# First cross-attention: the first 1,792 keys get a scale of their own and are made ahead of the values, and later keys are made two supers ahead

## The reference

```python
Qp = query @ Wq + bq
K = _l2norm(key @ Wk + bk)
V = value @ Wv + bv
Q = _l2norm(Qp)
... (16 heads of 8)
scores = jnp.einsum('bhqd,bhkd->bhqk', Q, K) * SCALE
attn = jax.nn.softmax(scores, axis=-1)
out = jnp.einsum('bhqk,bhkd->bhqd', attn, V)
out = out @ Wo + bo
x = out + Qp
mu = jnp.mean(x, axis=-1, keepdims=True)
var = jnp.mean((x - mu) ** 2, axis=-1, keepdims=True)
return (x - mu) / jnp.sqrt(var + LN_EPS) * ln_gamma + ln_beta
```

## Time and profile before

| | us |
|---|---|
| median of 3 runs | 663.24 (662.68 to 671.8) |
| the profiled execution | 663.12, span 661.3 |
| first and last exponential of this stage | start 34.25, end 99.60 |
| PE, DVE, ACT, POOL busy over the whole span | 513.6, 434.1, 299.6, 132.1 |
| mean granted clock of TensorE | 0.853 |

### The profile page before, as it was taken

How to read it: one execution, slowest core, us unless ns; L and a number is a source line. 1 busy time by engine, 2 the same in 40 slices (tenths; PEclk the granted TensorE clock), 3 DMA queues, 4 the chain that set the end, 5 groups by cost and what they waited for, 6 DMA issues and landing times. The chain is left out here.

```text
span 661.3 us, 11985 instructions
## 1 busy us (share of the span) xinstructions
PE 513.6 (78%) x4815; PEld 324.5 (49%) x4815; DVE 434.1 (66%) x828; ACT 299.6 (45%) x367; POOL 132.1 (20%) x197
## 2 busy tenths in 40 slices
PE   8799996788889997438995594782578488999857
PEld 5456673575355564313442263472456335556546
DVE  6744325856967955744999999925556596785243
ACT  2578881425557685111654560020112164768611
POOL 2111000000000000204688999400100000000000
PEclk9989997989899999556998587795569679999959
DMA  8364481563200000001022035052300150000000
GB/s 218 72 185 117 128 321 57 173 181 80 94 2 2 1 3 1 3 0 50 0 84 111 0 147 124 5 116 55 127 1 1 31 256 1 2 2 2 2 0 3
DMA packets 17674, 45.59 MB, mean 69 GB/s; under 512 B 4281, under 2 KB 13674, under 8 KB 16778
## 3 DMA queue, kind: packets, MB, share of 16 engines
q1 hardware_dynamic: 17556, 44.72, 22.3%
q0 software_dynamic: 64, 0.11, 0.1%
HBM read 34.28 MB, written 8.29 MB: 64 GB/s over the span
## 5 line engine op out<-in xcount | busy, mean ns | idle before, releaser
L251 POOL TENSOR_TENSOR rstd<-rstd,minus_half 64x1 f32<-64x1 f32 x20 | 11.8, 589 | 420.3 <-DVE rstd L259 420.3
L1497 ACT ACTIVATE ring<-psum,l3x_gain_columns 128x1024 f32<-128x1024 f32 x49 | 54.4, 1114 | 23.2 <-PE psum L1389 23.2
L1497 ACT ACTIVATE ring<-psum,l1x_gain_columns 128x1024 f32<-128x1024 f32 x49 | 54.4, 1114 | 22.4 <-PE psum L1389 22.4
L1403 PE MATMUL psum<-ring,values 128*32 128x128 f32 x1568 | 62.7, 279 | 0.4 <-ACT ring L1497 0.4
L934 ACT ACTIVATE ring<-psum,l0x_key_scale 128x1024 f32<-128x1024 f32 x49 | 52.1, 1114 | 8.2 <-PE psum L827 8.2
L1403 PEld LDWEIGHTS psum<-ring,values 128*32 128x32 f32 x1568 | 37.0, 109 | 28.1 <-issue 24.7
L1602 DVE TENSOR_REDUCE l1x_tops<-psum 128x1 f32<-128x448 f32 x64 | 36.7, 619 | 10.2 <-PE psum L1378 10.1
L1602 DVE TENSOR_REDUCE l3x_tops<-psum 128x1 f32<-128x448 f32 x64 | 36.7, 619 | 10.2 <-PE psum L1378 10.1
L3186 DVE MAX8 l2x_best<-values 128x8 f32<-128x6272 f32 x6 | 40.1, 6691 | 0.1
L3194 DVE MATCH_REPLACE8 values<-l2x_best,values 128x6272 f32<-128x6272 f32 x6 | 40.1, 6675 | 0.0
L827 PE MATMUL psum<-l0x_Q_stack,wide 96*128 96x256 f16 x196 | 29.8, 281 | 4.2 <-ACT ring L934 2.1
(11 more groups left out here) (778 smaller groups left out, 1080.7 us busy)
## 6 DMA issues: line engine op xcount, KB each, us to landing
wide<-keys_aside SPq DMA_DIRECT2D x54, 224.0 KB, 3.8
experts<-in_experts SPq DMA_DIRECT2D x1, 4608.0 KB, 13.5
experts<-in_experts SPq DMA_DIRECT2D x1, 4096.0 KB, 15.3
keys_aside<-ring SPq DMA_DIRECT2D x7, 448.0 KB, 2.5
keys_aside<-experts SPq DMA_DIRECT2D x6, 448.0 KB, 3.2
ring<-in_ctx_tiles SPq DMA_DIRECT2D x1, 2352.0 KB, 9.3
experts<-in_experts SPq DMA_DIRECT2D x1, 2048.0 KB, 7.8
ctx_t<-in_ctx_t SPq DMA_DIRECT2D x3, 672.0 KB, 7.4
```

What stands on the lines that cost most here:

```text
L1403: last = nc.tensor.matmul(ps[32 * quarter:32 * quarter + 32, O_BANK, 128 * half:128 * half + 128], mem.values[:, at:at + 32], probs[:, t % ...
L1497: nc.scalar.activation(probs[:, t % PROBS, :].rearrange("p (b n) -> p b n", b=2), ps[:, pair:pair + 2, :], ACT.Exp, scale=exp_gain[:, :]). ...
```

## The change

- `AHEAD` is 2: super u's tiles carry the keys of super u+2, and `norms(u+2)` comes at its tile 6 (before: at tile 0).
- Supers 0 and 1 get a power of two of their own, from the first piece of the context (`bounds(0)`, `power_of_two(0)`); supers 2 to 6 get the second, whose bound PE computes inside the loop, after tile 4's keys.
- Keys 0 and 1 come ahead of the values on PE, and keys 2 and 3 ahead of the last three; ACT and not DVE writes high parts of super 1.
- The queries' high rows of `Q_stack` are copied by 8 DVE copies; before, SP moved them by 8 transfers.
- Super 0's stack: SP issues 8 transfers of high parts as soon as those are there, POOL the 4 of low parts.
- From super 2 on DVE does, per super: high, low, high, low, `take_norms(u)`, `scale_keys(u)`; SP does `stack_keys(u)`, then `turn_norms(u)`.
- The bounds for level 1 move to the end of DVE's list, and on PE from t = 38 to t = 42.

The diff, cut to its core:

```diff
-    AHEAD = 3
+    AHEAD = 2
     blocks = [(g, block_row) for g in range(G) for block_row in range(3)]
-    OF_POOL = [(g, 2) for g in range(2)]
+    OF_POOL = [(g, 1) for g in range(G)]
...
+                stack_keys(0)
                 turn_norms(0)
-                stack_keys(0)
+                stack_keys(1)
                 turn_norms(1)
-                stack_keys(1)
                 load_pack(mem, sp, "l1x")
-                turn_norms(2)
-                stack_keys(2)
-                for u in range(3, SUPERS):
+                for u in range(2, SUPERS):
                     stack_keys(u)
                     turn_norms(u)
...
                     pe.wait_ge(squares_ready, 2 * u + 2)
                     if u:
                         pe.wait_ge(rows_ready, u)
+                    if u == 2:
+                        pe.wait_ge(*dve_done.at("key_gain1"))
...
-                values(0)
+                keys(0)
                 pe.wait_ge(*dve_done.at("xnT"))
                 nc.tensor.matmul(ps[0:T, 3, 192:320], xnT[:, :], mem.w(pack, "Wq"), start=True, stop=True)\
                     .then_inc(*pe_done.mark("Qp"))
+                keys(1)
+                values(0)
+                norms(0)
+                pe.wait_ge(*dve_done.at("bounds0"))
...
                 values(2)
-                pe.wait_ge(*dve_done.at("Qn"))
-                nc.tensor.transpose(ps[0:C, 3, 320:384], Qn[:, :], ident[0:T, 0:T]).then_inc(*pe_done.mark("QT"))
-                keys(0)
-                keys(1)
                 values(3)
-                norms(0)
+                keys(2)
+                keys(3)
                 pe.wait_ge(mem.loaded["ctx2"], 16)
...
                 norms(1)
-                keys(4)
                 pe.wait_ge(*act_done.at("Q_stack"))
-                pe.wait_ge(queries_stacked, 16 * 2 * G)
+                pe.wait_ge(*dve_done.at("Q_stack"))
...
-                        if j == 0 and u + 2 < SUPERS:
-                            norms(u + 2)
-                        if j in (2, 4) and u + AHEAD < SUPERS:
+                        if u + AHEAD < SUPERS and j in (2, 4):
                             keys(2 * (u + AHEAD) + j // 4)
-
-                pe.wait_ge(*dve_done.at("key_gain"))
+                        if u + AHEAD < SUPERS and j == 6:
+                            norms(u + AHEAD)
+                        if tile == 4:
+                            pe.wait_ge(*dve_done.at("bounds1"))
+                            pe.wait_ge(rows_ready, 2)
+                            nc.tensor.matmul(ps[:, 0, 0:C], mem.ones[0:CTX + 1, :], bound_rows[:, :], start=True,
+                                             stop=True).then_inc(*pe_done.mark("key_bound1"))
...
-                    if t == 38:
+                    if t == 42:
                         gains.pe_bounds(pe, 1)
...
-                for u in range(3):
-                    copy_values(u)
                 square(0)
                 square(1)
-                copy_values(3)
+                copy_values(0)
+                act.wait_ge(*dve_done.at("key_gain0"))
+                high(0)
+                high(1)
+                copy_values(1)
+                copy_values(2)
                 act.wait_ge(*dve_done.at("Q_parts"))
                 for g in range(G):
                     ins = nc.scalar.activation(Q_stack[64:96, g, :], Q_low[32 * g:32 * g + 32, :], ACT.Identity)
                 ins.then_inc(*act_done.mark("Q_stack"))
-                copy_values(4)
-                act.wait_ge(*dve_done.at("key_gain"))
-                high(0)
-                high(1)
-                copy_values(5)
+                copy_values(3)
                 square(2)
-                copy_values(6)
                 square(3)
-                square(4)
+                high(2)
+                high(3)
+                for u in range(4, SUPERS):
+                    copy_values(u)
...
-                pool.wait_ge(high_ready, 2)
+                pool.wait_ge(low_ready, 2)
...
+                def bounds(n, lo, hi):
+
+                    step(v.tensor_reduce(piece_tops[:, n:n + 1], mem.ctx_top[:, lo:hi], AX_X, ALU.max))
+                    v.tensor_scalar(bound_rows[:, :], keys_abs[:, :], piece_tops[:, n:n + 1], None, ALU.mult)\
+                        .then_inc(*dve_done.mark(f"bounds{n}"))
...
+                def power_of_two(n, row):
+                    dve.wait_ge(*pe_done.at(f"key_bound{n}"))
+                    step(v.tensor_reduce(bound[:, :], row, AX_X, ALU.max))
+                    step(v.tensor_scalar(power[:, :], bound[:, :], 1e-30, None, ALU.max))
+                    bits = power[:, :].bitcast(I32)
+                    step(v.tensor_scalar(bits, bits, EXPONENT_BITS, None, ALU.bitwise_and))
+                    step(v.reciprocal(inverse[:, :], power[:, :]))
+                    v.tensor_scalar(exp_gain[:, n:n + 1], power[:, :], 2.0 ** -13 / QUERY_GAIN, None, ALU.mult)
+                    v.tensor_scalar(key_gain[:, n:n + 1], inverse[:, :], 2.0 ** 13, None, ALU.mult)\
+                        .then_inc(*dve_done.mark(f"key_gain{n}"))
...
+                bounds(0, *CTX_PIECES[0])
...
+                power_of_two(0, ps[:, 3, 64:192])
                 dve.wait_ge(*pool_done.at("q_rsqrt"))
                 v.tensor_scalar(Qn[:, :], Qp[:, :], q_rsqrt[:, :], None, ALU.mult)\
                     .then_inc(*dve_done.mark("Qn"))
-                context_top(1)
+                dve.wait_ge(*dve_done.at("key_gain0"))
+                low(0)
...
+                low(1)
+                take_norms(0)
+                for g in range(G):
+                    for block_row in range(2):
+                        ins = v.tensor_copy(Q_stack[32 * block_row:32 * block_row + 32, g, :], Q_high[32 * g:32 * g + 32, :])
+                ins.then_inc(*dve_done.mark("Q_stack"))
+                low(2)
+                low(3)
+                context_top(1)
+                scale_keys(0)
+                take_norms(1)
...
-                dve.wait_ge(*dve_done.at("key_gain"))
-                low(0)
-                low(1)
-                step(v.tensor_scalar(exp_gain[:, :], power[:, :], 2.0 ** -13 / QUERY_GAIN, None, ALU.mult))
-                scale_keys(0)
-                for n in range(2, 2 * AHEAD):
-                    high(n)
-                    low(n)
-                    if n == 3:
-                        take_norms(1)
+                bounds(1, CTX_PIECES[0][1], SUPERS)
+                power_of_two(1, ps[:, 0, 0:C])
+                dve.wait_ge(*dve_done.at("key_gain1"))
                 scale_keys(1)
+                for u in range(2, SUPERS):
+                    for n in (2 * u, 2 * u + 1):
+                        high(n)
+                        low(n)
+                    take_norms(u)
+                    scale_keys(u)
                 dve.wait_ge(mem.loaded["rows"], 16)
                 step(v.tensor_tensor(residual[:, :], Qp[:, :], mem.row("l0x_bo"), ALU.add))
-                for u in range(2, SUPERS):
-                    if u == SUPERS - 1:
-                        gains.dve_rows(dve)
-                    take_norms(u)
-                    for n in range(2 * (u + AHEAD - 2), min(2 * (u + AHEAD - 1), HALVES)):
-                        high(n)
-                        low(n)
-                    scale_keys(u)
+                gains.dve_rows(dve)
```

More of the change, by code:

```diff
@@ L636, in stage_first_attention @@
     STACK = 96
-    AHEAD = 3
+    AHEAD = 2
     blocks = [(g, block_row) for g in range(G) for block_row in range(3)]
-    OF_POOL = [(g, 2) for g in range(2)]
+    OF_POOL = [(g, 1) for g in range(G)]
     OF_SYNC = [block for block in blocks if block not in OF_POOL]
     act_done.stage("Q_stack")
-    pe_done.stage("xnT", "Qp", "QT", "key_bound", "own", "projected")
-    dve_done.stage("var", "xn", "xnT", "q_sum", "Qn", "QT", "Q_parts", "bounds", "key_gain", "weighed",
-                   "OT", "out_var", "x")
+    pe_done.stage("xnT", "Qp", "key_bound0", "QT", "key_bound1", "own", "projected")
+    dve_done.stage("var", "xn", "xnT", "bounds0", "q_sum", "key_gain0", "Qn", "QT", "Q_parts", "Q_stack", "bounds1",
+                   "key_gain1", "weighed", "OT", "out_var", "x")
     pool_done.stage("rstd", "q_rsqrt", "out_rstd")
@@ L794, in _ @@
                     .then_inc(*pe_done.mark("Qp"))
+                keys(1)
+                values(0)
+                norms(0)
+                pe.wait_ge(*dve_done.at("bounds0"))
+                nc.tensor.matmul(ps[:, 3, 64:192], mem.ones[0:CTX + 1, :], bound_rows[:, :], start=True, stop=True)\
+                    .then_inc(*pe_done.mark("key_bound0"))
                 values(1)
+                pe.wait_ge(*dve_done.at("Qn"))
+                nc.tensor.transpose(ps[0:C, 3, 320:384], Qn[:, :], ident[0:T, 0:T]).then_inc(*pe_done.mark("QT"))
                 pe.wait_ge(mem.loaded["ctx1"], 16)
                 values(2)
-                pe.wait_ge(*dve_done.at("Qn"))
```

(21 more changed lines are left out.)

37 lines of the change are left out of this document (11 added, 26 removed).

## The result

The changed kernel took **680.47 us** (median of 4 runs, 677.39 to 684.56) against 664.88 of the kernel before beside it (4 runs): ratio 1.022, interval 1.011 to 1.033. Repeated on another chip it took 681.36 (10 runs) against 672.28 (19 runs): 1.024, 1.016 to 1.032. It is slower, since both intervals leave out 1; whether by more than the 2% that a measurement can tell from no change, they leave open. The forecast was 676.4, in a range of 667 to 683.

The account below looks back on a forecast made before the run. The ring, 13.4 us a super against PE's 9.6, was taken to set the pace: scale 1 at 35.9, five turns, last exponential at 112.9, 13.3 later; 663.1 + 13.3 = 676.4 us, range 667 to 683.

Parts of the forecast that it names:

- the ring: Loop from super 2: DVE, SP's transfers, POOL and DVE's scale wait in a circle, 13.4 us a super against PE's 9.6.
- the case that had the 0.60: The forecast itself: a ring of 12.9 to 13.9 us from a head as computed, chance 0.60.
- The head: Work ahead of the first exponential: it would come at about 26.5 us, 7.7 earlier than before.
- the two waits at the end: End of the head: waits for the last values and the first scores, some 0.9 us together.
- The query copies: Head, on DVE: 8 copies taken as 2 us together, done ahead of need, so costing nothing.
- the first stack: Head: super 0's transfers, SP's eight issued by 21.3 us with POOL's four beside them, costing nothing.
- The start of the ring: Super 1's scale on DVE, behind the second bound after tile 4's keys, at 35.9 us.
- the third rival's case: Late head: first exponential held to 30 us, each us late moving the end by one, 680 us; chance 0.12.
- The turn of the ring: One super's round from scale to scale in the loop: five legs summing to 13.4 us, bounds 12.5 to 14.8.
- The rival of shorter transfers: Loop: norm transfers could take 2.9 us, making the ring 12.2 and the time 670; chance 0.14.
- The end: From scale 6 at 102.9 us to the last exponential at 112.9, 13.3 later than before.
- a wrong sign of failure: Prediction is wrong if PE's idle time in the loop is put down to the stacks' transfers, not the exponentials.

Follow-up runs that it names:

- e1: The changed kernel run again, unedited: 681.36 us, 1.024 of the kernel before.
- e9: Changed kernel with the queries' high rows moved again by 8 SP transfers, not DVE copies: 680.68 us, 1.024 of the kernel before.
- e2: Changed kernel with DVE's highs and lows of super u+1 ahead of the scale of super u: 666.58 us, 0.995 of the kernel before.
- e5: Changed kernel with four useless DVE steps per super between a scale and the next high part: 689.37 us, 1.029 of the kernel before.
- e7: Changed kernel with POOL, not SP, issuing the two norm transfers from super 2 on: 668.30 us, 0.995 of the kernel before.
- e12: Changed kernel with second bound at tile 2, keys at tiles 0 and 2, norms at 4, ACT's squares two tiles earlier: 675.92 us, 1.017.
- e11: e10 plus keys at tiles 0 and 2, norms at tile 4, ACT's squares two tiles earlier: 664.35 us, 0.995 of the kernel before.
- e8: Changed kernel with the edits of e2 and e4, and super 2's norm transfers ahead of its stack: 671.74 us, 1.008 of the kernel before.
- e3: Changed kernel with SP's norm transfers ahead of the stack from super 2 on: 685.77 us, 1.019 of the kernel before.
- e4: Changed kernel with PE's second bound at tile 2 instead of tile 4: 676.89 us, 1.010 of the kernel before.
- e6: e2 with the useless DVE steps of e5 ahead of each super's high and low parts: 674.67 us, 1.014 of the kernel before.
- e10: Changed kernel with the edits of e7 and e4 together: 670.44 us, 1.005 of the kernel before.

## Why the prediction was right

The mechanism is the one forecast: the chain of the ring, with nothing overlapped, longer than PE's work. The end of the stage agrees more closely than its terms do, and the case that had the 0.60, a ring of 12.9 to 13.9 from a head as computed, did not come quite as stated: the ring was 12.87 and the head 2.6 late.

**The head.** Forecast first exponential 26.5, measured 29.09. Two terms were short: `key_gain0` at 16.2, not 15.1, since PE's bound began at 14.54 (DVE waited 1.42 for it); and the two waits at the end, 0.9 in the sum, took 1.17 and 1.16. The query copies took the 2 us chosen, and the first stack, issued by POOL until 22.3 and by SP until 23.0, was hidden:

```profile
20.52 2.04 DVE L1057 COPY l0x_Q_stack<-l0x_Q_high 32x256 f16<-32x256 f16 x8
```

**The start of the ring.** Forecast 35.9, measured 40.15. The head gave 2.6 of the 4.2. Of the rest 1.4 is TensorE at half clock as the loop began, which the sum had only at the end: from the first exponential to scale 1 it was 11.1 here, 9.7 in e1 without it, 9.4 in the sum. The granted clock was 0.50 from 31.4 to 34.2 here and 1.00 in e1. DVE stood waiting for the bound all the while:

```profile
39.00 0.29 DVE L1009 TENSOR_REDUCE l0x_bound<-psum 128x1 f32<-128x128 f32 x1 [6.35 <-PE psum L851]
```

The first weighing matmuls:

```profile
32.29 1.94 PE L834 MATMUL psum<-ring,values 128*32 128x128 f32 x32
...
36.03 1.08 PE L834 MATMUL psum<-ring,values 128*32 128x128 f32 x32
```

This is nearly the third rival's case, a late head (30, for 680). Its rule, each us late is a us on the end, is borne out by e9.

**The turn of the ring.** Forecast 13.4, measured 12.5, 13.5, 12.5, 12.4 and 13.4, mean 12.87: in the bounds of 12.5 to 14.8. The term that was most too long is the transfer to DRAM, 3.3 in the sum, 2.53, 3.61, 2.50, 2.48 and 2.49 here, mean 2.7. Pieces took 1.3 to 1.65, mean 1.4 where 1.6 stood, and the norm transfers 3.9 to 5.2, mean 4.3 where 4.1 stood. The rival of shorter transfers counted on the norm transfers (2.9), which were not shorter; the one to DRAM was, by 0.6 of the 1.2 that the rival needed.

**The end.** 8.6 from scale 6 to the last exponential, not 10.0. The half clock that the sum priced at 1.4 came (0.51 from 104.4 to 106.2), but ACT took four exponentials on end there, 104.79 to 109.01, since PE had made their scores while it waited, and was idle only 0.99 behind them. So +4.2 at the start, 2.6 less in the five turns and 1.4 less behind: the end came at 113.13, forecast 112.9. That it agrees to 0.2 is luck, errors of 4.2 and 4.0 that cancel; the mechanism, not the exact sum, is what e2, e5, e7 and e12 show. I had said that PE's idle time would not be put down to the stacks; 10.4 us of it was, since a stack lands at about the time of the scale. That was a wrong sign of failure, for the same ring delays both: the stack waits for the same low parts. Nor was PE idle 3 us ahead of each super: in the five turns it was idle 1.8, 4.1, 0.7, 3.0 and 3.1, for at half clock, in parts of the last four, its work took longer.

**What was said to hide.** From the second turn on PE, ACT and their keys are no part of the ring: e12 has them two tiles earlier and keeps the pace. The early head was not lost in the closed ring: e9, with a later head, ended later by as much and more. The slower pace outweighed it. With the ring mostly open, in e11, it shows in the end: 6.0 earlier than before the change at the first exponential, 5.3 at the last.

**Behind the stage.** I had put everything that follows as unchanged. It wasn't in the profiled execution. The stretch from the next stage's first POOL step to the end of level 1's loop, and the rest, before and after:

```profile
105.40:262.60 157.20, 135.90 (x1463) 85.32 (x1463) 111.77 (x263) 87.12 (x101) 3.68 (x7) 0.95 0.20 56
262.60:661.30 398.70, 284.11 (x2181) 179.96 (x2181) 273.66 (x459) 143.96 (x189) 111.84 (x173) 0.79 0.15 47
```

```profile
118.90:284.00 165.10, 145.00 (x1463) 92.07 (x1463) 112.06 (x263) 87.23 (x101) 3.67 (x6) 0.89 0.20 54
284.00:682.40 398.40, 284.12 (x2181) 180.00 (x2181) 273.71 (x459) 143.97 (x189) 111.78 (x173) 0.79 0.15 47
```

The columns are the stretch, its length, busy time (and count) of PE, PEld, DVE, ACT and POOL, TensorE's granted clock, and the transfers' share and GB/s. The same 1,463 matmuls took 9.1 us more at a mean clock of 0.89 than at 0.95, so the stretch is 7.9 longer; what follows is the same to 0.3. A longer time behind the stage is not the changed kernel's alone: from the end of the last exponential to the end of the span it is 561.7 to 562.3 in the profiles of before, e2, e7 and e8, 563.6 to 564.1 in e3 and e12, and 568.3 to 570.4 in the changed kernel's, e1, e4, e5, e6, e9, e10 and e11. The forecast's 676.4 was worked out from an execution of 663.1. Of the changed kernel's four runs two took 677.4, close to it, and the median is 4.1 above it, though the stage ended as forecast. Why the matmuls behind the stage get the lower clock in one execution and not in another is open: no run isolates it.

## What to carry to other kernels

Where engines with queues in order hand work round, write the circle down: for each wait, what stands behind it on that queue, and whether it leads back. If it does and that sum is longer than the work, the sum of the legs is the pace, whatever the busy shares say, and one early item at another place (a scale one super later, or a small transfer on another queue) opens it. An order that frees one resource may tie another: e3 and e8 moved a small transfer forward, and a large one had to wait behind it. A head that is shortened moves the start of the loop behind it and not its pace; here the pace cost 18.7 us and the head gave 5.2.

## What the runs showed of the hardware

- Two norm transfers of 3.5 KB together took 2.5 to 3.2 from POOL's issue to POOL's start where no pieces were issued shortly before (ten cases in e7, e10 and e11, nine of them under 2.9), and 4.7 to 6.0 where the three pieces had been issued 0.2 to 0.6 earlier (five cases). In the changed kernel, where SP issues both, 1.3 to 1.65 behind the pieces, 3.9 to 5.2. No run moved this distance by itself. The Trainium skill, "DMA: Bandwidth & Descriptors", section on the anatomy of one DMA, has a fixed 2.0 us plus the bytes, for transfers that GpSimd issues. The 2.6 estimated from it in the prediction fits the first kind and none of the others.
- The transfer of 448 KB of keys to DRAM took 2.48 to 2.53 from its issue to that of the pieces in four of the five turns of the changed kernel, 3.61 in the other, and up to 4.4 in e5 (42.85 to 47.25). In that last case the DMA engines were 0.55 busy with 208 GB/s until 45.0 and 0.04 busy behind it: the bytes had gone in half the time. What the rest was spent on is open. The 3.1 estimated in the prediction from the same page's section lies between the short cases and the long.
- TensorE came back at a granted half clock (0.50) behind some stretches with waits: the same 32 matmuls 1.94 and 1.08. In the loop's start it cost 1.4 us (first profile of the changed kernel against e1), behind scale 6 some 3 (11.5 to the end in e4, 8.6 in e1). It came or not in executions of the same kernel.
